# A gated delta-net layer with a quantised feed-forward: sums of squares by products with a 128x2 selector, the residual added by VectorE, and another order of steps

## The reference, cut to what matters

```python
q = silu(conv(xn @ Wq)); k = silu(conv(xn @ Wk)); v = silu(conv(xn @ Wv))   # 4-tap causal conv
gk = -exp(A_log) * softplus(xn @ Wgk + dt_bias); beta = sigmoid(xn @ Wb + b_b)
q = q * rsqrt(sum(q*q, -1) + 1e-6) * DK**-0.5      # the sums of squares of this case
k = k * rsqrt(sum(k*k, -1) + 1e-6)
for each row t:
    S = S * exp(gk[t]); delta = (v[t] - k[t] @ S) * beta[t]
    S = S + outer(k[t], delta); o[t] = q[t] @ S
o = rmsnorm(o) * g_norm_weight * g * sigmoid(g)    # g = xn @ Wg
x = x + o @ Wo + fp4_linear(silu(gate) * up, w_down)
```

## Time and profile before

| what | value |
|---|---|
| median of three runs | 3064.13 us (3057.14 to 3064.31) |
| the profiled execution's own time | 3054.66 us |
| its span | 3052.9 us |
| PE busy | 2657.3 us (87%) |
| DVE busy | 2522.1 us (83%) |
| ACT busy | 2201.2 us (72%) |
| POOL busy | 1625.6 us (53%) |
| mean granted TensorE clock | 0.939 of full speed |

### The profile page before, as it was taken

How to read it: one execution, slowest core, us unless ns; L and a number is a source line. 1 busy time by engine, 2 the same in 40 slices (tenths; PEclk the granted TensorE clock), 3 DMA queues, 4 the chain that set the end, 5 groups by cost and what they waited for, 6 DMA issues and landing times.

```text
span 3052.9 us, 83158 instructions
## 1 busy us (share of the span) xinstructions
PE 2657.3 (87%) x25361; PEld 2131.6 (70%) x25487; DVE 2522.1 (83%) x7140; ACT 2201.2 (72%) x6626; POOL 1625.6 (53%) x2418
## 2 busy tenths in 40 slices
PE   4789898889888898988989889899888988889986
PEld 3577777777767677776777667777677776767775
DVE  7888898888788887888878888888888888888872
ACT  3677777777677777776767767777777777777774
POOL 3565554565544556445654446554456654456651
PEclk8899999999999999999999989999999999999997
DMA  2111011111011111111110111101111101111101
GB/s 64 22 34 35 15 33 35 35 24 35 16 34 35 24 35 25 24 35 24 35 36 14 35 29 30 36 16 34 36 27 32 35 16 34 35 24 35 33 16 23
DMA packets 319431, 91.35 MB, mean 30 GB/s; under 512 B 283057, under 2 KB 310001, under 8 KB 318961
## 3 DMA queue, kind: packets, MB, share of 16 engines
q1 hardware_dynamic: 318960, 85.59, 13.5%
HBM read 46.76 MB, written 38.80 MB: 28 GB/s over the span
## 4 chain that ended last, share of the span: by engine, by line
PE 54%; DVE 25%; issue 11%; ACT 4%; POOL 3%; DMA 1%; DVEq 1%; SPq 0%; ACTq 0%; POOLq 0%
DVE KQ L914 6%; PE ring L1382 5%; PE ring L1228 5%; DVE UP L1010 5%; PE bank_o L1349 4%; PE ring L1211 4%; PE ring L1178 3%; PE ring L1169 3%; PE bank_e L1318 3%; PE bank_e L1331 3%; PE bank_e L1335 2%; PE ring L1241 2%; DVE ssr L979 2%; PE bank_o L1355 2%; PE bank_e L1326 2%
## 5 line engine op out<-in xcount | busy, mean ns | idle before, releaser
L614 POOL TENSOR_TENSOR laneA<-laneA,laneT 96x30 f32<-96x30 f32 (+14 forms) x960 | 520.3, 542 | 75.3
L611 POOL TENSOR_TENSOR laneT<-laneA 96x30 f32<-96x30 f32 (+14 forms) x960 | 498.9, 520 | 68.0
L914 DVE SCALAR_TENSOR_TENSOR KQ<-ring,ckq,KQ 128x255 f32<-128x255 f32 (+2 forms) x1152 | 460.5, 476 | 17.5 <-DVE nabs L949 6.5
L914 DVE SCALAR_TENSOR_TENSOR vc<-ring,cvv,vc 128x255 f32<-128x255 f32 (+2 forms) x1152 | 462.8, 476 | 3.9 <-ACT vc L718 0.8
L598 POOL TENSOR_TENSOR sqk<-sse,phalf 128x8 f32<-128x8 f32 x96 | 157.4, 1639 | 576.9 <-DVE sse L984 576.9
L1010 DVE SCALAR_TENSOR_TENSOR UP<-ring,cj,gm 128x256 f32<-128x256 f32 x768 | 327.2, 478 | 26.7 <-PE ring L1195 14.9
L1055 DVE SCALAR_TENSOR_TENSOR V<-bank_o,negG,V 128x128 f32<-128x128 f32 x384 | 134.3, 350 | 202.9 <-PE bank_o L1355 146.3
L592 POOL TENSOR_TENSOR gm<-g,mle 128x512 f32<-128x512 f32 x192 | 197.6, 1051 | 179.0 <-DVE UP L1010 165.9
L1211 PE MATMUL ring<-xnT,wv 128*128 128x256 f32 x768 | 231.8, 430 | 62.7 <-DVE KQ L914 53.9
L1169 PE MATMUL ring<-gm,mgt 128*128 128x512 f32 x384 | 218.7, 654 | 59.1 <-DVE UP L1010 58.3
L1178 PE MATMUL ring<-xnT,wqk 128*128 128x256 f32 x768 | 237.2, 446 | 36.6 <-issue 34.5
(11 more groups left out here) (164 smaller groups left out, 7902.6 us busy)
## 6 DMA issues: line engine op xcount, KB each, us to landing
to_lanes<-UP SPq DMA_DIRECT2D x128, 96.0 KB, 2.7
laneA<-to_lanes SPq DMA_DIRECT2D x32, 384.0 KB, 3.5
from_lanes<-laneA SPq DMA_DIRECT2D x32, 384.0 KB, 3.0
UP<-from_lanes SPq DMA_DIRECT2D x128, 96.0 KB, 3.0
turned_lanes<-laneX SPq DMA_DIRECT2D x32, 288.0 KB
N<-turned_lanes SPq DMA_DIRECT2D x96, 96.0 KB, 2.7
xin<-_attn_hidden_states_dram SPq DMA_DIRECT2D x32, 128.0 KB, 2.7
xres<-_attn_hidden_states_dram SPq DMA_DIRECT2D x32, 128.0 KB, 3.2
```

Source lines behind the costliest of these rows:

```text
L611: link(nc.gpsimd.tensor_tensor(t, A[:, 0:m, j:j + 1].broadcast_to([LANES, m, n]), A[:, j:j + 1, j + 1:BLK].broadcast_to([LANES, m, n]), AL ...
L614: link(nc.gpsimd.tensor_tensor(w, w, t, ALU.add))
L914: ins = nc.vector.scalar_tensor_tensor(acc[:, n, s:T], src[:, n * T:n * T + T - s], wt(n)[:, TAPS - 1 - s:TAPS - s], acc[:, n, s:T], ALU.m ...
```

## The change

Four things change.

1. `QT`, `QTr`, `QN` are gone. `SS` squares keys and queries of a pair of heads on ScalarE, straight from SBUF into `sq`. `QT` (even pair) and `QU` (odd pair) each multiply four 128x128 blocks of `sq`, as the stationary operand, with `sel`, a 128x2 matrix of ones and zeros, so that two columns of a bank hold the sums of the two heads. `SSr` reads all 16 columns of the bank when both pairs are in.
2. `YO` no longer multiplies `xres` with the identity; `YOr` adds `xres` to the bank where it copied it.
3. The list `ORDER` is another one (266 steps for 272), and with it the banks of the ring.
4. `XN` on ScalarE has one more wait, for a `GP` product two passes back.

```diff
-KEEP = ((("ZBr", 0, 1), ("XQ0", 0, 1)), ...
+KEEP = ((("SS", 0, 1), ("QT", 0, 1)), (("SS", 1, 1), ("QU", 0, 1)), ...
 ORDER = (
-    ("QK", 0, 1), ("VT", 3, 0), ("ZB", 0, 1), ("VPs", 4, 0), ("VTr", 3, 0), ("STORE", 0, 0), ("QK", 1, 1),
+    ("QK", 0, 1), ("LANEP", 7, 0), ("ZB", 0, 1), ("VT", 3, 0), ("ZBr", 0, 1), ("VT", 2, 0), ("QKr", 0, 1),
...
-READER = {"QK": "QKt", "VP": "VPt", "GP": "OG", ("FU", 1): "FUm"}
+READER = {"QK": "QKt", "QT": "SSr", "VP": "VPt", "GP": "OG", ("FU", 1): "FUm"}
...
-                    if kind == "QT":
+                    if kind == "SS":
 
                         if a >= 2 or not zero(i):
-
-                            act.wait_ge(s_sums, cnt(i, NP, a - 1) if a >= 2 else cnt(i - 1, NP, a + 5))
-                        nc.scalar.activation(sq[:, a % 2, :, :].rearrange("p g d -> p (g d)"), b[:, :], ACT.Square)\
-                          .then_inc(read("QT", a), 1)
+                            if a % 2 == 0:
+                                act.wait_ge(s_even, cnt(i, NG, a // 2))
...
+                        act.wait_ge(s_kq, cnt(i, NP, a + 1))
+                        nc.scalar.activation(sq[:, a % 2, :, :], kq()[:, a, :, :], ACT.Square).then_inc(s_sq, 1)
...
-                    if kind == "QN":
-                        dve.wait_ge(read("QT", a), rv(i, "QT", a))
-                        nc.vector.tensor_reduce(ssr[:, :, :, 2 * a:2 * a + 2],
...
-                        dve.wait_ge(s_sums, cnt(i, NP, 2 * a + 2))
-                        nc.vector.tensor_scalar(sse[:, :, :, 4 * a:4 * a + 4], ssr[:, :, :, 4 * a:4 * a + 4],
+                        dve.wait_ge(full("QT", a), rv(i, "QT", a))
+                        nc.vector.tensor_scalar(sse[:, :, :, 4 * a:4 * a + 4],
+                                                bank("QT", a)[:, 0:16].rearrange("p (w t h) -> p w t h", w=2, t=NT),
...
-                        link(nc.vector.tensor_copy(yb[:, :, :].rearrange("p t n -> p (t n)"), b[:, 0:T]))
+                        link(nc.vector.tensor_tensor(yb[:, :, :].rearrange("p t n -> p (t n)"), b[:, 0:T],
+                                                     xres[:, :, :].rearrange("p t n -> p (t n)"), ALU.add))
...
-                                ins = nc.tensor.transpose(b[:, o:o + P], KQ[:, a, w, t * P:(t + 1) * P], ident[:, :])
-                        ins.then_inc(full("QT", a), 1)
+                                o = 4 * (w * NT + t) + 2 * j
+                                ins = mm(b[:, o:o + 2], sq[:, j, w, t * P:(t + 1) * P], sel[:, :], start=True, stop=True)
+                        ins.then_inc(s_even if j == 0 else full("QT", a), 1)
...
-                        mm(y[:, 0:T], ident[:, :], xres[:, :, :].rearrange("p t n -> p (t n)"), start=True, stop=False)
```

More of the change, by code:

```diff
@@ L59 @@
-    ("QT", 0, 1), ("QK", 4, 1), ("DDg", 2, 1), ("VTr", 5, 0), ("VTr", 4, 0), ("VPr", 1, 1), ("QTr", 0, 1),
-    ("DDg", 3, 1), ("DD", 0, 1), ("QKs", 2, 1), ("VPt", 1, 1), ("QKs", 3, 1), ("TFETCH", 0, 0), ("VP", 2, 1),
-    ("QKr", 4, 1), ("QT", 1, 1), ("FETCH", 0, 0), ("DDr", 0, 1), ("DD", 1, 1), ("QKt", 4, 1), ("VPr", 2, 1),
-    ("QT", 2, 1), ("QTr", 1, 1), ("QTr", 2, 1), ("DD", 2, 1), ("MY", 0, 0), ("MY", 1, 0), ("QN", 0, 1),
-    ("DDr", 1, 1), ("VPt", 2, 1), ("DDr", 2, 1), ("MY", 2, 0), ("MYr", 0, 0), ("VPt", 0, 1), ("QK", 5, 1),
@@ L64 @@
-    ("MZ", 0, 0), ("QKr", 5, 1), ("QT", 3, 1), ("MZr", 0, 0), ("MYr", 1, 0), ("DD", 3, 1), ("QN", 1, 1),
-    ("DDr", 3, 1), ("SSr", 0, 1), ("QTr", 3, 1), ("CJ", 0, 1), ("MY2", 0, 0), ("GR", 0, 1), ("QKt", 5, 1),
-    ("GRr", 0, 1), ("GRr", 1, 1), ("QKs", 4, 1), ("MY2r", 0, 0), ("QN", 2, 1), ("MZ", 1, 0), ("QKs", 5, 1),
-    ("MZr", 1, 0), ("GR", 1, 1), ("QN", 3, 1), ("GRr", 2, 1), ("SSr", 1, 1), ("MYr", 2, 0), ("GR", 2, 1),
[10 rows of a table removed]
-    ("GP", 0, 0), ("MZ2r", 2, 0), ("SQ", 11, 0), ("LANEP", 0, 1), ("FUm", 1, 1), ("VPs", 1, 1), ("LANEP", 1, 1),
[12 rows of a table removed]
@@ new lines @@
+    ("VT", 4, 0), ("VP", 1, 1), ("GCr", 0, 1), ("QKs", 0, 1), ("SS", 0, 1), ("VTr", 5, 0), ("QKr", 2, 1),
+    ("DDg", 1, 1), ("QKs", 1, 1), ("QT", 0, 1), ("VPr", 0, 1), ("TSTORE", 0, 0), ("SS", 1, 1), ("QKt", 2, 1),
+    ("VPr", 1, 1), ("TFETCH", 0, 0), ("QK", 3, 1), ("VTr", 4, 0), ("VP", 2, 1), ("VPr", 2, 1), ("QU", 0, 1),
+    ("VPt", 1, 1), ("DDg", 2, 1), ("DD", 0, 1), ("QK", 4, 1), ("SSr", 0, 1), ("QKs", 2, 1), ("VPt", 2, 1),
+    ("FETCH", 0, 0), ("SS", 2, 1), ("DD", 1, 1), ("DDr", 0, 1), ("MY", 0, 0), ("MY", 1, 0), ("DDr", 1, 1),
@@ new lines @@
+    ("QKr", 3, 1), ("DD", 2, 1), ("MYr", 0, 0), ("QKr", 4, 1), ("MZ", 0, 0), ("VPt", 0, 1), ("DDr", 2, 1),
+    ("QKt", 3, 1), ("DDg", 3, 1), ("CJ", 0, 1), ("MYr", 1, 0), ("MZr", 0, 0), ("GR", 0, 1), ("GRr", 0, 1),
+    ("GRr", 1, 1), ("GR", 1, 1), ("XR", 0, 0), ("MZ", 1, 0), ("DD", 3, 1), ("MZr", 1, 0), ("MY2", 0, 0),
+    ("LN", 0, 2), ("DDr", 3, 1), ("MY2r", 0, 0), ("DDg", 4, 1), ("QKt", 4, 1), ("GRr", 2, 1), ("QK", 5, 1),
+    ("GRr", 3, 1), ("DDg", 5, 1), ("MX", 1, 0), ("QKs", 3, 1), ("XQ0", 0, 1), ("QKr", 5, 1), ("DD", 4, 1),
[3 rows of a table added]
@@ new lines @@
+    ("GRr", 5, 1), ("GRr", 6, 1), ("QT", 2, 1), ("DD", 5, 1), ("QU", 2, 1), ("GRr", 7, 1), ("SSr", 2, 1),
+    ("GR", 4, 1), ("CJ", 2, 1), ("DDr", 5, 1), ("GR", 5, 1), ("MY", 2, 0), ("GRr", 8, 1), ("GRr", 9, 1),
+    ("VPs", 1, 1), ("XQ", 0, 1), ("GRr", 10, 1), ("MYr", 2, 0), ("VPr", 3, 1), ("GRr", 11, 1), ("XQr", 0, 1),
+    ("SE", 5, 0), ("SO", 5, 0), ("VPt", 3, 1), ("MZ", 2, 0), ("VPs", 2, 1), ("LN2", 0, 2), ("SO", 6, 0),
+    ("MZr", 2, 0), ("FU", 0, 1), ("SE", 6, 0), ("MX", 2, 0), ("MZ2r", 1, 0), ("FUr", 0, 1), ("VT", 0, 1),
@@ L675, in iteration @@
                     if kind == "XN":
+                        if not early(i):
+                            split(act, full("XN", 0), full("GP", 5))
+                            act.wait_ge(full("GP", 5), rv(i - 2, "GP", 5))
                         nc.scalar.activation(xnT[:, par(), :], b[:, 0:T], ACT.Copy).then_inc(read("XN", 0), 1)
```

53 lines of the change are left out of this document (30 added, 23 removed), and 37 rows, old and new, of the table ORDER.

## The result

The changed kernel takes 3159.78 us (median of four, 3154.15 to 3162.09), the kernel before 3064.22 us (3057.14 to 3066.81). The ratio is 1.0313, 95% interval 1.0291 to 1.0335: slower by 3.1%, where 1.3% faster had been forecast and where the range ended at 3085.

A forecast was written before the change was run, and what follows sets the result against it. VectorE was taken to bound part one, TensorE part two. Per period 92.85 + 2.0 - 3.0 = 91.85 us, likeliest -1.3; over 31 periods -40 us, 3064 to 3024 us, range 2970 to 3085.

The forecast's parts named there:

- Part one, VectorE's chain: From `z` to VectorE's first state read: 43.04 us, changed steps sum to +2.0, so 45.0 us.
- What TensorE pays for the sums ... taken at nothing: Part one: selector passes cost TensorE 1.7 to 2.6 us more a pass, covered by its free time, so 0.
- I expect this slow spell to vanish in half of the passes: Behind the first state read, in part two: TensorE's slow clock goes in half the passes, -0.8 us (bounds 0 and -1.7).
- New waits ... I charge 0.5 us; the bounds are 0 and 1.7 us: Part two: waits around `VPt` 5 and for GpSimd's power between the last `OS` and `OG` 4, +0.5 us.
- The 46.8 us: Forecast length of part two, VectorE's first state read to the next `z`: 49.81 us with -3.0.
- the residual's -0.43 us: Part two, TensorE's chain: the residual product with the identity goes, -0.43 us; the addition replacing the copy taken at 0.
- one less on TensorE in part two only: Premise from busy times and waits: a microsecond less counts on VectorE in part one only, on TensorE in part two only.
- Rival 4: First group of each pass: `SSr` waits for a late, half-clock `QU`, VectorE stands about 1 us; 3055 us, chance 0.10.
- Rival 3: End of part one: ScalarE's two more table switches count in full, +1.3 us per period, 3104 us; chance 0.17.
- Rival 1: Part two: clock keeps its slow spell, new waits at their upper bounds; about 0 per period, 3064 us; chance 0.13.
- my bonus of 0.3: Part one: fewer gaps before VectorE's six removed reductions, taking the likeliest from -1.0 to -1.3 us per period.

The follow-up runs named there:

- the wide selector: The changed kernel with a selector of 64 columns in place of 2, the same sums and number of passes; 3109.8 us, 1.018.
- e11: The kernel before with four idle products (eight passes) of 2 columns ahead of the transposes of each QT; 3209.4 us, 1.051.
- e12: The kernel before with four idle products (eight passes) of 64 columns ahead of the transposes of each QT; 3160.8 us, 1.036.
- e16: The kernel before with two idle products of 64 columns (four passes) for each QT; 3094.1 us, 1.009.
- e4: The changed kernel's new order with the sums of the kernel before, and the residual on TensorE again; 3349.0 us, 1.096.
- e15: e13 with GpSimd's lane steps LANEP 2, 3, 4 put behind the powers OS 0, 1, 2; 3145.5 us, 1.026.
- e3: Sums by the 2-column selector and residual on VectorE, put into the order of the kernel before; 3263.8 us, 1.062.
- e17: e15 with MY 0, MY 1 and their reads moved behind GR 0; 3133.8 us, 1.022.
- e13: The changed kernel with a 64-column selector, DD 5 behind DD 4 and DDr 5 behind DDr 4 (two table loads fewer a pass); 3093.4 us, 1.010.
- e10: e9 with DD 5 behind DD 4 and DDr 5 behind DDr 4 as well; 3125.2 us, 1.021.
- e9: The changed kernel with a 64-column selector and GpSimd's lane step LANEP 2 behind OS 0; 3102.4 us, 1.012.

## Why the prediction was wrong, step by step

**Part one, VectorE's chain: right in number, in part by luck.** Forecast 45.0 us. With the wide selector, where the clock is not in the way, it is 44.1 us, +2.3 on the mean before, where I had +2.0. VectorE's busy time in it grew by 0.9 us only (39.6 to 40.5; 1.1 in the changed kernel): some of its small instructions became faster, others slower (last section), 0.8 us less in all. That hid that its stalls had not stayed as they were. `SSr` takes 170 ns from the bank as from SBUF, so 0 was the right end.

**"What TensorE pays for the sums ... taken at nothing": this step failed.** It failed twice. First, I priced a pass by its spacing, 0.09 to 0.11 us, and that was right: the eight that start at 1480.90 us are followed by the next product at 1481.71, 0.10 us each. But nearly at full clock TensorE's work in part one grew from 34.0 to 38.9 us (with the wide selector), and passes there are not hidden: 24 idle ones, as many as the change adds, cost the kernel before 0.9 us a period. Busy shares said 9 us free; VectorE's stalls sit where TensorE is late, not where it is free. Part one grew there by 1.2 us; what stays of the +2.3 above, when VectorE's 0.9 us more of work is taken off, is 1.4 us. That the two are the same thing is likely and not shown.
Second, and this is the larger part in part one, the passes are 2 columns wide. The earlier trace rows shows their neighbours' time and nothing of what they do to the clock. The same passes at 64 columns give back 3.9 of the 6.1 us in part one, and the whole slow spell of 36 to 48 us behind `z`.

**"I expect this slow spell to vanish in half of the passes": wrong in its reason.** The spell behind the first state read did go, and in more passes than forecast: it is in 16 of 27 before and in none of 27 in the changed kernel. But by `e11`, `e12` and `e16` its going was worth nothing in the kernel before, where I had -0.8 us; and a longer one opened ahead of it, among the very steps that I had moved there to close the gap. I had read the earlier trace rows as "TensorE idle, so slow". The Trainium skill, page "TensorE: Matmul & The Clock Gate", section "Part 1: The HAM clock gate (the "warmup" mystery)", says likewise that the clock follows how busy the engine has been of late. The traces agree for gaps (`e4`, `e15`). For narrow products, which the profile counts as busy, busy time did not tell: in `e3` 5 us in which TensorE was busy throughout were followed by 0.50.

**"New waits ... I charge 0.5 us; the bounds are 0 and 1.7 us": this step failed too, and -2.7 us for -3.0 in part two is luck.** Of the new waits the one for the power is 2.3 us a pass in the changed kernel and 4.0 once part one is short; then part two is 50.4 us, 0.6 less than before and not 3.0. What had been shortened ahead of GpSimd's chain came back as a wait for it, so the slow clock in part one covered this second error. The 46.8 us were reached only in `e15` and `e17` (46.3 and 46.0), and were paid for in part one. Two terms don't hold by themselves either: the residual's -0.43 us and the slow spell's -0.8 us are nothing in the kernel before (ratio 1.0004 for the first; part two as long as ever without the second). So "one less on TensorE in part two only" was a premise that busy shares (48.59 of 49.8 us) had suggested and no run bears out for the whole loop: the passes without its edge got shorter, those with it longer.

**Rivals.** Rival 4 (`SSr` waits for `QU` at half clock) named the right place and mechanism. I priced it at 1 us for one wait and 3055 us; measured are 67.5 us of waits for the sums, 30.5 for `GR` behind them, and 23.5 for the state read behind both, over the whole span. Its source was missing: that the passes themselves bring on the slow clock. Rival 3 (ScalarE's table loads) gave the nearest time, 3104 us, for a reason that carries 0.5 to 0.8 us a period, if that: the gain of `e13` is not in part one. Rival 1 was right that the clock stays slow, and wrong on where. The range missed since no case in it had the clock fall further than it already had.

**The sum of it.** -1.0 forecast without my bonus of 0.3; +3.4 measured. Of the 4.4 us between them, 3.9 is the slow clock in part one. The wide selector recovers 1.4 to 1.6 of it net (42 to 50 us over 31 periods), as GpSimd's chain takes the rest in part two. So the slow clock costs 1.4 to 1.6 us a period in this order; in one whose part two doesn't wait for GpSimd I estimate up to 3.9. The other 2.7 to 3 us stay with the clock up: the kernel with the wide selector is 53 us over its kernel before, +1.7 a period for my -1.0. Nearly all of that is part two, -0.6 for -3.0. The bonus of 0.3, for fewer gaps before VectorE's work, went the other way: its idle time in part one is 3.6 us with the wide selector and 7.3 in the changed kernel, for 2.2 before.

What stays open: what gives the time back at the loop's edge when TensorE has less to do in part two; why undoing the residual costs 37 us in the changed kernel; why 16 columns are slightly slower than 2; and why `e10` is slower than `e9` and `e13`, its two halves.

## What to carry to other kernels

When work moves to TensorE, ask how wide its products are and not only how many: here passes that the profile counts as busy brought the clock down, and then every product behind them paid. Free time of an engine in a stretch does not cover what is added to it, if another engine waits for it at the end of each of its steps; a cheap test is to add idle passes to the old kernel and time it. And a step that two kernels' orders share with a chain round the loop (here lanes and powers on GpSimd) has to be costed from the chain's own start, since what is shortened ahead of it comes back as a wait. Last, when an error has been found and undone, see whether the forecast holds then: here the kernel was still slower than before.
